# First expert layer: seven block products for eight in half of the second product, squares on ScalarE, no clamp

## What is computed

```python
b, l, d = x.shape                      # 1, 1250, 768
logits = x.mean(axis=1) @ router_w.T + router_b
top_v, top_i = jax.lax.top_k(logits, 2)            # 2 of 4 experts for the whole batch
gates_k = jax.nn.softmax(top_v, axis=-1)
h = einsum('bld,edh->belh', x, w1) + b1            # 1536 hidden channels
h = stack([_ACTS[i](h[:, i]) ...])                 # gelu, silu, v*tanh(softplus(v)), gelu
out = einsum('belh,ehd->beld', h, w2) + b2
y = einsum('be,beld->bld', gate, out) + x
return layernorm(y) * ln_g + ln_b
```

## Time and profile before

| | |
|---|---|
| Median of 3 runs | 2633.81 us (2632.14 to 2635.1) |
| The profiled execution | 2630.19 us |
| Its span (first to last instruction) | 2628.4 us |
| PE busy | 2555.2 us (97%) |
| DVE busy | 1587.2 us (60%) |
| ACT busy | 769.6 us (29%) |
| Mean granted clock of PE | 0.995 |
| Expert layer 0, PE from its first matmul to its last | 1014.5 to 1631.2 us |

### The profile page before, as it was taken

One profiled execution on the slowest core, in us unless ns is written; L12 is line 12 of the kernel. 1 busy time (PEld: TensorE's weight loads), 2 busy tenths in 40 slices (PEclk: granted clock), 3 DMA queues, 4 the chain that ended last, 5 costly groups with the idle time before them and its releaser, 6 DMA issues.

```text
span 2628.4 us, 26650 instructions
## 1 busy us (share of the span) xinstructions
PE 2555.2 (97%) x10594; PEld 1813.6 (69%) x10594; DVE 1587.2 (60%) x2708; ACT 769.6 (29%) x1291; POOL 347.7 (13%) x197
## 2 busy tenths in 40 slices
PE   7999999999999997999999999999999999999999
PEld 4667667558965996777777775565755786556676
DVE  4456471779948996987888998254342561341322
ACT  1043342006732863222222221430002331332000
POOL 0888888000000000000000000000000000000000
PEclk9999999999999998999999999999999999999999
DMA  9232313543020406000120003200450100213201
GB/s 257 26 44 14 50 2 50 143 145 123 20 80 20 116 1 215 1 0 1 72 102 0 24 24 115 70 1 1 115 164 18 37 1 1 63 37 126 87 24 59
DMA packets 139168, 160.74 MB, mean 61 GB/s; under 512 B 96618, under 2 KB 108484, under 8 KB 137516
## 3 DMA queue, kind: packets, MB, share of 16 engines
q1 hardware_dynamic: 68323, 158.60, 19.4%
q0 software_dynamic: 70720, 0.43, 2.8%
HBM read 122.75 MB, written 35.87 MB: 60 GB/s over the span
## 4 chain that ended last, share of the span: by engine, by line
PE 51%; DVE 7%; ACT 2%; issue 1%; DMA 0%; SPq 0%; DVEq 0%; ACTq 0%
PE psum L521 51%; DVE arena L1863 2%; DVE arena L1865 1%; DVE arena L1864 1%; PE psum L532 0%; DVE arena L1856 0%; ACT arena L1126 0%; ACT arena L1131 0%; ACT arena L1015 0%; DVE arena L1519 0%; DVE arena L1929 0%; DVE arena L1361 0%; DVE arena L1862 0%; DVE arena L1855 0%; DVE arena L1888 0%
## 5 line engine op out<-in xcount | busy, mean ns | idle before, releaser
L521 PE MATMUL psum<-arena 128*125 128x384 f32 (+12 forms) x9762 | 2454.4, 413 | 34.8 <-DMA arena<-in_ffn_w 7.1
L521 PEld LDWEIGHTS psum<-arena 128*125 128x125 f32 (+3 forms) x9762 | 1719.8, 188 | 745.5 <-issue 136.7
L2278 POOL DMA_INDIRECT count_matrix<-arena x170 | 343.0, 2018 | 121.1 <-DVE arena L1458 59.7
L1863 DVE RECIPROCAL arena<-arena 128x500 f32<-128x500 f32 x60 | 196.7, 3278 | 2.1
L1613 DVE CUSTOM_DVE_ANT_0 arena<-arena 125x1250 bf16<-125x1250 bf16 (+1 forms) x100 | 139.2, 1458 | 12.9 <-DMA arena<-source_rows 8.3
L2288 POOL MEMSET arena<- 125x60 f32 x1 | 0.2, 208 | 1039.4 <-PE psum L521 1039.4
L1697 DVE TENSOR_TENSOR arena<-arena 125x1250 f32<-125x1250 f32 x80 | 116.3, 1453 | 13.7 <-ACT arena L1108 13.6
L1105 ACT ACTIVATE arena<-arena 125x1250 f32<-125x1250 f32 x80 | 106.9, 1336 | 56.7 <-PE psum L521 56.5
L1700 DVE SCALAR_TENSOR_TENSOR arena<-arena 125x1250 f32<-125x1250 f32 x80 | 116.9, 1461 | 2.8
L1015 ACT ACTIVATE arena<-psum 128x250 f32<-128x250 f32 (+1 forms) x102 | 40.6, 494 | 231.4 <-PE psum L532 230.9
L1248 ACT ACTIVATE arena<-psum,arena 128x250 f32<-128x250 f32 x120 | 49.3, 465 | 198.6 <-PE psum L521 198.6
(11 more groups left out here) (226 smaller groups left out, 1435.0 us busy)
## 6 DMA issues: line engine op xcount, KB each, us to landing
arena<-in_ffn_w SPq DMA_DIRECT2D x3, 4608.0 KB, 14.9
residual<-arena SPq DMA_DIRECT2D x30, 336.0 KB
arena<-residual SPq DMA_DIRECT2D x30, 336.0 KB
arena<-target_rows SPq DMA_DIRECT2D x12, 610.4 KB
arena<-in_gat_w SPq DMA_DIRECT2D x3, 2304.0 KB, 10.5
arena<-residual SPq DMA_DIRECT2D x10, 672.0 KB
residual<-arena SPq DMA_DIRECT2D x10, 672.0 KB
count_matrix<-arena SPq DMA_DIRECT2D x2, 3125.0 KB, 26.9
```

Of the source, the lines that this page charges most:

```text
L521: return pe.matmul(o, lhsT, rhs, start=start, stop=stop, skip_group_check=share)
L1863: now(dve.reciprocal(t_, t_))
L2278: pool.indirect_dma_start(counts[k], bass.IndirectOffsetOnAxis(ap=IDX_I[0:T, c:c + 1].bitcast(U32), axis=0), COUNT_I[0:T, c:c + 1], None, ...
```

## The change

**Second product.** The first six of the twelve channel blocks are multiplied as two-by-two blocks: tiles (2) x groups of three channel blocks (2) on the left, groups of channel blocks (2) x column halves (2) on the right. Seven block products of three matmuls each take the place of eight; the other six channel blocks are multiplied as before ("rest", six matmuls a bank). So 45 products of 125x384 a unit for 48. The block products go through banks in an order in which one bank, a, is accumulated further and is read by DVE in between: three partial readings of bank a and one of bank b, each reported by down_read, for each of which PE waits before it goes on with that bank. DVE makes seven additions onto XN a unit for four. DVE also makes the sums of hidden channels (five instructions of 125 to 375 columns a unit, hidden_sums) and, once an expert, four sums of weight blocks of 128x1152 (w2_sums, behind ratio 3 of u = 1 and of u = 6).

**Activation.** There is no clamp. ACT takes the exponential with a per-expert factor (1/2 or 1) and squares it with a per-expert offset (0 or 1), both in place, in a buffer for two steps. DVE takes min with 1e30 and adds 1, takes the reciprocal, multiplies and adds constants, and multiplies by the hidden value: four instructions for seven with the clamp. Gelu works in place in HB, behind the end of all six ratios of its unit.

**Order on DVE.** Per u: ratio 0 to 4 (add_bias behind ratio 2 for u = 1 to 5), partial addition 1 of unit u - 1, ratio 5, partial addition 2, bank d, partial addition 3, the mixing instruction, bank b, the sums, partial addition 4, the residual of a pair, banks c and a.

**Loads.** The last of six blocks of WQ and three bias rows of the next mixer are loaded at t = 9 behind bank b of the last unit; the rest of WQ at t = 7 as before.

The core of the diff:

```diff
+            def down0(u):
...
+                product(1, bank_a, True).then_inc(down_filled, 1)
+                pe.wait_ge(hidden_sums, u + 1)
+                pe.wait_ge(w2_sums, u // 5 + 1)
+                product(5, bank_b, True).then_inc(down_filled, 1)
+                rest(1, 1, bank_d, True)
+                pe.wait_ge(down_read, n + 1)
+                product(6, bank_a).then_inc(down_filled, 1)
+                pe.wait_ge(down_read, n + 2)
+                product(3, bank_b, False, False)
+                rest(0, 1, bank_b)
+                pe.wait_ge(down_read, n + 3)
+                product(7, bank_a).then_inc(down_filled, 1)
+                product(2, bank_c, True, False)
+                rest(0, 0, bank_c)
+                pe.wait_ge(down_read, n + 4)
+                product(4, bank_a, False, False)
+                rest(1, 0, bank_a)
...
                 def expo(i):
-                    act.wait_ge(clamped, 6 * u + i + 1)
-                    act.activation(EB[:, 2 * i:2 * i + 2, :], TB[:, 2 * i:2 * i + 2, :], ACT.Exp).then_inc(expd, 1)
+                    n = 6 * u + i
+                    if n >= 2:
+                        act.wait_ge(exp_read, n - 1)
+                    act.wait_ge(a_drained, A_AT[("f1", u, i)] + 1)
+                    x = EB[n % 2]
+                    act.activation(x, HB[u % 2][:, 2 * i:2 * i + 2, :], ACT.Exp, scale=SCL[:, e:e + 1]).then_inc(act_step, 1)
...
+                    act.activation(x, x, ACT.Square, bias=MISH[:, e:e + 1]).then_inc(expd, 1)
...
             def ratio(u, i):
...
+                dve.tensor_scalar(t_, EB[n % 2], BIG, 1.0, ALU.min, ALU.add).then_inc(exp_read, 1)
+                dve.wait_ge(exp_read, n + 1)
+                now(dve.reciprocal(t_, t_))
+                now(dve.tensor_scalar(t_, t_, c(NCK), c(KO), ALU.mult, ALU.add))
+                ins = dve.tensor_tensor(t_, t_, h, ALU.mult)
...
             for u in range(11):
                 if u < 10:
+                    for i in range(5):
+                        ratio(u, i)
+                        if u > 0 and u <= 5 and i == 2:
+                            add_bias(u - 1)
+                        if (u, i) in ((1, 3), (6, 3)):
+                            weight2_sums(u // 5)
+                if u > 0:
+                    down = {x: bank(("f2", u - 1, x)) for x in "dbca"}
+                    add_part(u - 1, 1, "a", 0, 0)
+                if u < 10:
+                    ratio(u, 5)
+                if u > 0:
+                    add_part(u - 1, 2, "b", 1, 1)
+                    dve.wait_ge(down_read, 4 * u - 2)
+                    add_bank(u - 1, "d", 1, 1)
+                    add_part(u - 1, 3, "a", 0, 1)
```

## The result

The changed kernel took 2701.09 us (median of 4 runs, 2699.02 to 2703.33), the kernel before 2632.97 in the same session: ratio 1.0264, 95% interval 1.0251 to 1.0277. It is slower by 68 us. The forecast was 2701, from a sum of 67.6. The profiled execution has a span of 2697.0 us, 68.6 more than before.

What follows compares the result with a forecast made beforehand. PE's matmuls were taken to bound the stage, with new waits for DVE's readings. Passes summed 23.9 + 25.0 + 8.1 + 13.2 - 2.6 = 67.6 us, giving 2701; 8-in-10 range 2680 to 2721.

Steps and rivals of the forecast that it cites:

- A ratio, 4.94: On DVE, four instructions per ratio take 4.94 us from start to start, against 7.0 with the clamp.
- Start of ratio 0, 13.58: In a steady pass, DVE starts ratio 0 at 13.58 us, behind ACT's exponential and a Square of 0.62.
- The clock, 1.7 in seven passes: After PE's wait of some 3.6 us, 3.4 us at half clock lose 1.7 us of products per pass.
- u = 2 to 5, +6.25 each: Bias additions ahead of partial addition 1 add waits of 2.8 and some 3.6 us; each pass loses 6.25 us.
- u = 1, +23.9: DVE starts ratio 0 27.5 us into the pass; PE idles 22 us for the weight sums; pass loses 23.9.
- weight sums hidden: Rival: DVE comes to the weight sums earlier than the order shows; 21 us less, 2680; chance 0.05.
- u = 6, +8.1: Weight sums behind ratio 3 end at 38.8 us, PE waits 6.6; the pass loses 8.1 us.
- u = 7 to 9, +4.4 each: Passes with nothing else on DVE: PE waits 0.9 and 3.6 us, plus 1.7 slow clock; each loses 4.4.
- Loads at nothing: WQ's last block at t = 9 costs nothing, as residual work comes relatively earlier; without that cover up to 5 us.
- clock stays at 2.4 GHz: Rival: no slow clock behind the waits, seven passes lose 1.7 us less; 2689 us; chance 0.10.
- Square needs a table of its own: Rival: a table load on ACT adds 1.28 us ahead of ratio 0 in nine passes; 2713 us; chance 0.03.
- The other side: Rival: DVE's readings come in time, PE loses nothing and 30 products are gained; 2614 us; chance 0.04.

Runs made afterwards that it cites:

- filled_waits: Changed kernel with 4 or 5 useless products put ahead of PE's waits for readings 1 and 2 in steady passes; 2687.97 us, ratio 1.0215 to before.
- sums_early: Changed kernel with weight sums moved to u = 0 and behind ratio 1 of u = 6, bias rows earlier in u = 0; 2698.85 us, ratio 1.0256 to before.
- bank_c_early: both_early with bank c added ahead of the residual of a pair in u = 7 to 9; 2615.40 us, ratio 0.9944 to before.
- no_reciprocal: Changed kernel with the reciprocal left out of each ratio, so values are wrong; 2627.03 us, ratio 0.9982 to before.
- both_early: Changed kernel with weight sums and bias rows moved earlier and DVE's partial bank readings placed between the ratios; 2618.84 us, ratio 0.9955 to before.
- readings_early: Changed kernel with DVE reading the partial banks between ratios, not behind ratios 4 and 5, weight sums left in place; 2656.13 us, ratio 1.0099 to before.
- longer_ratio: Changed kernel with one more DVE instruction (times 1, plus 0) in each ratio; 2722.18 us, ratio 1.0348 to before.

## Why the prediction was right

Step by step, in its own terms:

- **A ratio, 4.94.** Right to the hundredth, the first instruction too: 0.42 us, and 0.46 to the next start; the price of L1855's row would have been 0.12 too much. The Trainium skill (VectorE: DVE Perf Modes, "Mode 2x_2P — use both read ports for one tensor") gives two elements a cycle for one float32 tensor from SBUF, and the trace agrees in part: the price estimated with it holds here, while L1915, which has one tensor too but reads its constants one a partition, takes 0.54.
- **Start of ratio 0, 13.58.** 13.74: exponential and Square are 0.71 each (0.708 and 0.712 by the groups of the trace), for 0.62 and 0.62. The bound of 0.1 for the exponential held; for Square I had named none. It costs 0.2 us a pass.
- **Restart of PE, 0.15.** 0.05. The two errors nearly cancel.
- **The clock, 1.7 in seven passes.** The size of one stretch is right and its place isn't fixed. Behind the second wait it costs nothing at u = 3, 1.5 to 1.7 in most passes, and 2.7 at u = 9, where the stretch is the long one. filled_waits takes it away and finds 11.0 us in the stage and 13 in the whole time, 11.9 forecast.
- **u = 2 to 5, +6.25 each.** +6.6, 4.9, 6.5, 6.6: 24.6 for 25.0.
- **u = 1, +23.9.** +24.0, PE idle 22.44 for 22.4. But the text gave the wait to the weight sums, as if to move them were to win it; sums_early shows that the length of DVE's queue is what counts (moving them and the bias rows won 7.2 us in this pass, where the rival "weight sums hidden" said 21). The sum of the pass was made in this way, and so was right.
- **u = 6, +8.1.** +8.5.
- **u = 7 to 9, +4.4 each.** +4.7, +4.5, and +5.4 by PE's timeline (bank 0 of u = 9 is drained at 1609.03, so the pass begins at 1603.97; from 1648.56, 30 products and 2.7 of slow clock end it near 1670.7).
- **u = 10, -2.6.** From 1670.7 to the turned tiles at 1699.98 is 29.3; before, from 1599.4 by the steady pace to 1631.0, 31.6: -2.3.
- **Loads at nothing.** Right for the changed kernel: the last block of WQ goes out at 1697.94, and the mixer starts with the same 0.73 us as before. In bank_c_early the cover was gone and the wait came, 1.7 us, within the 5 named.

Sum of the passes by the profile: 24.0 + 24.6 + 8.5 + 14.6 - 2.3 = 69.4 for 67.6; the spans differ by 68.6. That it comes so near is in part luck: the slow clock that was counted at u = 3 and did not come (1.7) offsets the longer one of u = 9 (1.0) and part of the later start of ratio 0.

Of the rivals, "clock stays at 2.4 GHz" is excluded by the windows, "Square needs a table of its own" by ACT's timeline, "weight sums hidden" by the 22.44. The other side is not excluded as a mechanism: it said that DVE must read in time, and put the point at ratios of 3.2 us. no_reciprocal confirms that the length of a ratio decides. But the rival's 2614, and the 4.1 us for no change, were worked out for a steady pass: u = 1 starts late whatever the ratio, and with ratios of 1.63 us it still takes 10.9 us more than before (102.6 for 91.7), so that the whole time is 2627. That the order alone could do the same, with ratios as they are, was not in the prediction; both_early shows it.

## What to carry to other kernels

Nothing hid the waits of the engine that sets the time here, so before an algorithm with fewer products is taken, the releasing instruction has to be placed on the other engine's queue, with all that stands ahead of it; the order of work on DVE alone decided between 1.026 and 0.995. When a wait is ended by a short instruction, the cause is the queue ahead of it: moving that instruction moved the name in the row and won only the time of what was moved (7.2 us of the 22.4 at u = 1, for 5.4 and 1.7 us of instructions). Work that comes free of a deadline (ratios, whose result is needed a pass later) belongs behind work that has one (readings of a bank that PE is to go on with).

## What the runs showed of the hardware

- The length of a wait of PE alone did not decide whether the clock fell. In the stage every wait of 3.29 us and more, in all the profiles, was followed by work at 1.2 GHz. Of the shorter ones, 1.94 us (changed kernel, u = 2) and 2.11 us (bank_c_early) were; 2.96 us at u = 4 and 5 of the changed kernel (product 6 took 2.20 us there, granted clock 1.00) and 2.48 us in no_reciprocal were not, nor were 1.78, 1.58 and 1.03 us. Elsewhere in the program even 1.48 us was (both_early, 0.50 from 478 to 480 us).
- The stretch was mostly 3.4 us, but 6.8 at u = 9 of the changed kernel, behind a wait of 3.38. Behind the 22.46 us of readings_early it went on for 5.8 us of work (to 1109.8).
- With two waits close together it could be longer: in sums_early, around a wait of 2.96 us and, one product later, one of 1.38 us, the clock was low from 1234.6 to 1244.8 us. It was not so each time: in longer_ratio, around 5.24 and 1.84 us at u = 2, it was back at 1.00 before the second wait ended.
- Products of no use inside a wait keep the clock at 2.4 GHz: 51 of them made the program 13 us faster.
- ACT's exponential and Square of 128x500 with a scale or offset read from memory, one a partition, take 0.71 us; the exponential with neither took 0.62.
- PE goes on 0.05 us after the DVE instruction that it waits for has ended.
